# A graph network's count-matrix builder: tiles taken in an order in which heavy and merged ones alternate

## The reference

```
# layer 0: messages weighted by three Gaussians of the edge's attributes, averaged by destination
xj    = x[src] @ g                                   # E x (3*64)
msg   = einsum(xj.reshape(E,3,64), gauss)            # gauss: E x 3
aggr  = segment_sum(msg, dst) / max(count(dst), 1)
x     = layernorm(x + silu(aggr + x @ root_w + bias + x))
# layer 1: two SAGE convolutions over the same edges
h     = relu(x @ W_self1 + (segment_sum(x[src], dst) / deg) @ W_neigh1 + b1)
x     = layernorm(x + h @ W_self2 + (segment_sum(h[src], dst) / deg) @ W_neigh2 + b2)
```

## Time and profile before

| | us |
|---|---|
| median of 3 runs | 7653.07 (7649.23 to 7657.9) |
| the profiled execution | 7651.4 |
| its span, first to last instruction | 7649.6 |
| busy in the span: PE / DVE / POOL / ACT | 5050.4 / 4374.6 / 3367.5 / 2714.0 |
| granted TensorE clock, mean | 0.832 |

### The profile page before, as it was taken

One profiled execution on the slowest core, in us unless ns is written; L12 is line 12 of the kernel. 1 busy time (PEld: TensorE's weight loads), 2 busy tenths in 40 slices (PEclk: granted clock), 3 DMA queues, 4 the chain that ended last, 5 costly groups with the idle time before them and its releaser, 6 DMA issues.

```text
span 7649.6 us, 144672 instructions
## 1 busy us (share of the span) xinstructions
PE 5050.4 (66%) x35195; PEld 4048.2 (53%) x35196; DVE 4374.6 (57%) x15088; ACT 2714.0 (35%) x8317; POOL 3367.5 (44%) x3146
## 2 busy tenths in 40 slices
PE   1565655555566666655555555555545899999999
PEld 1223333333344444444444444444425899999999
DVE  5668888767677777665656656566543322222222
ACT  3113333334444444455555555555532000000000
POOL 5024555555666666666666666666630000000000
PEclk9558888877788888777778888788775899999999
DMA  2001222212222222222222222222230799999998
GB/s 71 28 24 49 68 68 68 67 51 87 78 96 83 87 91 90 90 90 91 90 90 91 91 90 90 73 90 90 91 85 3 298 381 383 381 367 385 385 384 344
DMA packets 258352, 1082.32 MB, mean 141 GB/s; under 512 B 140102, under 2 KB 144230, under 8 KB 194406
## 3 DMA queue, kind: packets, MB, share of 16 engines
q1 hardware_dynamic: 142806, 968.66, 32.8%
q0 software_dynamic: 100352, 102.96, 6.9%
q10 hardware_dynamic: 14902, 8.11, 0.5%
HBM read 751.67 MB, written 327.81 MB: 141 GB/s over the span
## 4 chain that ended last, share of the span: by engine, by line
PE 39%; DVE 20%; issue 14%; DVEq 13%; POOL 5%; DMA 5%; ACT 4%; ACTq 1%; SPq 1%; POOLq 0%
PE pw L970 21%; PE pw L800 9%; DVE rE L1269 5%; POOL rE L512 5%; DVEq L1302 3%; DMA tab<-tab_d 3%; DVEq L1472 3%; PE pw L825 3%; DVE rE L1267 2%; DVE rE L1329 2%; PE pw L772 2%; ACT rE L559 1%; DVE rE L1395 1%; PE pw L937 1%; ACT sca L575 1%
## 5 line engine op out<-in xcount | busy, mean ns | idle before, releaser
L512 POOL DMA_INDIRECT rE<-in_x,idx x3136 | 3365.4, 1073 | 2262.7 <-issue 2092.9
L800 PE MATMUL pw<-rE 128*128 128x193 f32 x7824 | 1775.9, 391 | 921.5 <-DVE rE L1329 885.9
L598 ACT CAST rB<-pw 128x792 bf16<-128x792 f32 x1568 | 1259.6, 814 | 2903.6 <-PE pw L825 1489.4
L800 PEld LDWEIGHTS pw<-rE 128*128 128x128 f32 x7824 | 1623.7, 233 | 1130.5 <-DVE rE L1329 1061.5
L559 ACT ACTIVATE rE<-rE,cols 128x64 f32<-128x64 f32 x4704 | 1254.5, 344 | 8.2 <-DMA tab<-tab_d 8.2
L825 PE MATMUL pw<-rE 128*128 128x396 f16 x3840 | 804.1, 357 | 577.8 <-DVE rE L1269 576.8
L1269 DVE TENSOR_SCALAR rE<-iperm,gr 128x392 f16<-128x392 f16 x3840 | 1052.1, 314 | 0.0
L825 PEld LDWEIGHTS pw<-rE 128*128 128x128 f16 x3840 | 368.8, 103 | 954.4 <-DVE rE L1269 681.1
L970 PE MATMUL pw<-rB,rA 128*128 128x192 bf16 x9604 | 810.8, 246 | 0.1
L970 PE MATMUL pw<-rE,rA 128*128 128x192 bf16 x9604 | 810.4, 246 | 0.1
L970 PEld LDWEIGHTS pw<-rB,rA 128*128 128x128 bf16 x9604 | 790.8, 98 | 1.6
(11 more groups left out here) (256 smaller groups left out, 2626.6 us busy)
## 6 DMA issues: line engine op xcount, KB each, us to landing
rA<-count SPq DMA_DIRECT2D x392, 1568.0 KB, 8.5
count<-rB SPq DMA_DIRECT2D x98, 3136.0 KB
rE<-in_x,idx POOLq DMA_INDIRECT x3136
cols<-cols_d SPq DMA_DIRECT2D x98, 64.0 KB
cols_d<-rA SPq DMA_DIRECT2D x3, 1568.0 KB, 5.2
rA<-in_edge_attr ACTq DMA_DIRECT2D x1, 4608.0 KB
out<-gcol ACTq DMA_DIRECT2D x97, 32.0 KB, 5.8
count<-rB SPq DMA_DIRECT2D x8, 224.0 KB, 2.0
```

The lines of the kernel that those rows point to most:

```text
L512: pool.indirect_dma_start(out=gath[:, s, u * CB + b, :], out_offset=None, in_=x, in_offset=bass.IndirectOffsetOnAxis(ap=idx[:, s, u * CB + ...
L598: act.copy(stage[:, s, :, j * 2 * W:(j + 1) * 2 * W].rearrange("p h (w n) -> p w h n", w=2), pu[j % 3][:, :, 0:CW].rearrange("p w (h n) -> ...
L800: ins = pe.matmul(sums[side][:, 0:AW], onehot[:, side, bb, :], wgath[:, side, bb, :], start=(bb == 0), stop=(bb == CB - 1))
```

## The change

It makes a list `ORDER` of the tiles and lets every engine go through it by place q. In it the 14 heavy tiles alternate with the first 14 merged ones: 0, 1, 2, 48, 3, 49, 4, ... 60, 15, 61, then the single tiles 16 to 47, then the merged tiles 62 to 97. So `q` now sets the slot and the semaphores' values, and `t` the tile. VectorE, TensorE and ScalarE have a loop with a merged and a heavy tile in one turn, 13 times. SyncE's loops are written out, with fixed addresses. Merging needs its own input tile `gm`, since a heavy tile uses `gr` at the same time. `merge_ahead` goes from unit 4 to unit 6 of the tile before, and ScalarE's copies from units 6 to 9 to units 7 to 10. A merged tile behind a heavy one waits at its units 0 to 3 for more of the ring to be free. Two loops of VectorE, that over the single tiles and that over the last merged ones, get `head_slot` 16, which loads the loop's first instruction at slot 16 of a fetch block of 256 instructions; before, 22 and 1 padding instructions stood ahead of them.

```diff
+NI = T4 - DT - 1
+QC = DT + 2 + 2 * NI
+QM = QC + TM - T4
+ORDER = list(range(DT + 1)) + [t for i in range(NI) for t in (TM + i, DT + 1 + i)] + [TM + NI] \
+    + list(range(T4, TM)) + list(range(QM, 98))
...
-            tile_counts(DT, 2, late=False)
-            with dve.Fori(0, T4 - DT - 1, 1) as i:
-                tile_counts(i + (DT + 1), 2)
-
-            dve.wait_ge(a_used, T4 * NU + RU)
-
-            for _ in range(22):
-                dve.sem_inc(s_tick[3], 1)
-            with dve.Fori(0, TM - T4, 1) as i:
-                tile_counts(i + T4, 1)
-            dve.wait_ge(a_pair, TM * NU)
-            merge_ahead(TM)
-            merge(TM)
-            for _ in range(1):
-                dve.sem_inc(s_tick[3], 1)
-            with dve.Fori(0, NT - 1 - TM, 1) as i:
-                merged_counts(i + TM)
-            merged_counts(NT - 1, True)
+            tile_counts(DT, DT, 2, late=False, s=0, following=(TM, 0))
+            with dve.Fori(0, NI, 1) as i:
+                merged_counts(i * 2 + (DT + 1), i + TM, s=1)
+                tile_counts(i * 2 + (DT + 2), i + (DT + 1), 2, s=0, following=(i + (TM + 1), i + 1))
+            merged_counts(QC - 1, TM + NI, s=1)
+            with nc.Fori(0, QM - QC, 1, engines=[dve.engine], head_slot={dve.engine: 16}) as i:
+                tile_counts(i + QC, i + T4, 1)
+            dve.wait_ge(a_pair, QM * NU)
+            merge_ahead(QM, QM, QM - TM, 0)
+            merge(QM - TM)
+            with nc.Fori(0, NT - 1 - QM, 1, engines=[dve.engine], head_slot={dve.engine: 16}) as i:
+                merged_counts(i + QM, i + QM, behind=1, following=(i + (QM + 1), i + (QM + 1 - TM)))
+            merged_counts(NT - 1, NT - 1, s=1, behind=1)
...
-                        dve.wait_ge(a_used, t * NU + (n + 1))
+                        free = n + 1 if behind < 2 else max(n + 1, min(n + 3, 4))
+                        dve.wait_ge(a_used, q * NU + free)
...
+            def merge_between(n, q, following, other):
+                t, m = following
+                if n == 6:
+                    merge_ahead(q + 1, t, m, other)
+                if n == NU - 2:
+                    merge(m)
```

More of the change, by code:

```diff
@@ L384, in _ @@
             sp.sem_inc(a_col, 1)
-            for s in range(2):
-                load_cols(s, s)
+            for q in range(2):
+                load_cols(q)
             for u in range(U):
                 sp.wait_ge(a_g[0][u], 16 * CB)
[L389 to L409, removed]
+            load_idx(2)
             def tile_of(c, t):
@@ L415, in _ @@
                 sp.sem_inc(a_st[s], 1)
[L416 to L420, removed]
-                if end:
-                    after(part, n - 4, 0)
-                    after(part, n - 3, 1, rows=False)
-                    for s in range(2):
-                        after(part, n - 2 + s, s, True, False)
+            for q in range(NT):
+                part = max(k for k, (base, _) in enumerate(PARTS) if ORDER[q] >= base)
+                sp.wait_ge(a_evac, q * NU + (NU + 2))
+                sp.wait_ge(a_bnd, q + 1)
+                sp.dma_start(tile_of(count[part][0], ORDER[q] - PARTS[part][0]), stage[:, q % 2, None, 0:NT, :]).then_inc(a_st[q % 2], 16)
+                if q + 2 < NT:
+                    sp.wait_ge(a_list, q + 1)
+                    load_cols(q + 2)
+                if q + 3 < NT:
+                    for u in range(U):
+                        sp.wait_ge(a_g[1 - q % 2][u], 16 * CB * ((q + 1) // 2 + 1))
+                    load_idx(q + 3)
             sp.wait_ge(e_clr, 1)
@@ L1397, in merged_counts @@
                         if n == 1:
-                            listed(t - 1, slot_of(t + 1) if not isinstance(t, int) else 1 - t % 2)
-                            base_of(t)
+                            listed(q - 1, other)
+                            base_of(q, t)
                         if n % (NU // U) == 1:
-                            prepare(t, s, u)
-                        if n == 4 and not last:
-                            merge_ahead(t + 1)
-                        if n == NU - 2 and not last:
-                            merge(t + 1)
+                            prepare(q, s, u)
+                        if following is not None:
+                            merge_between(n, q, following, other)
                 for k in range(2):
```

157 lines of the change are left out of this document (87 added, 70 removed).

## The result

| | before | after |
|---|---|---|
| median (lowest to highest), us | 7653.09 (7649.23 to 7657.9) | 7420.99 (7416.69 to 7424.71) |
| ratio to before, 95% interval | | 0.9696 [0.9679, 0.9713] |
| the profiled execution, us | 7651.4 | 7416.69 |
| VectorE's `wbase`: heavy and first 14 merged tiles | 871.8 + 671.4 = 1543.2 | 1395.3 |
| first seven single tiles | 426.0 | 402.6 |

The five stretches say where: 148 us in the pairs (forecast: 55 there and 16 further on), 60 in the last merged tiles (forecast: 4), 23 in the first single tiles (forecast: 0), 7.5 in the other single ones.

The account below looks back on a forecast made before the run. VectorE was taken to set the pace in the heavy stretch, GpSimd in the merged one. 7651.4 - 71 (moved merged tiles) - 4 (later `merge_ahead`) = 7576 us, as a median 7578; range 7485 to 7642.

Parts of the forecast that it names:

- VectorE sets the pace in the pairs, GpSimd keeps up: Pairs of heavy and merged tile: 111 us of VectorE against 98.8 us of GpSimd, 12 us to spare.
- A merged tile costs 44 us beside a heavy one: The 14 moved merged tiles: 687 us leave the end, 616 come in beside heavy tiles, 71 us saved.
- once per pair as it was per heavy tile: 0: Loop branch in the pairs: about 2.1 us per turn, paid as often as before, so no change.
- its upper end: Moved merged tile's highest price: 53 us, today's 48.0 plus a 5.2 us wait like the longest at L1394.
- the borders: Rival: turns between heavy and merged tiles cost 8.5 us extra, 110 us against 75 gained: 7688 us; chance 0.07.
- its second rival: Part of the merged tiles' waits closes beside heavy ones: 39 us per tile, 141 us saved, 7512 us; chance 0.16.
- part of the waits closes: Rival: merged tiles at 39 us beside heavy ones, 141 us saved, 7512 us; chance 0.16.
- The last 36 merged tiles: Later `merge_ahead` there: GpSimd sets the pace, so 4 us saved, within bounds of 0 and 45 us.
- Loop heads 0: VectorE's single and last merged loops: new position gains up to 23 us or loses 48; taken as 0.
- The rival of the cached loop: Single loop begun at slot 16 keeps its head cached, branch free: 23 us more saved, 7555 us; chance 0.06.
- Borders cost more than they bring: Rival: branch and TensorE wait add 8.5 us in each of 13 pair turns, 7688 us; chance 0.07.
- the forecast's 71: Saving from moving 14 merged tiles beside heavy ones: 687 us leave the end, 616 come in.

Follow-up runs that it names:

- a_fewg: The changed kernel with only four of a chunk's eight gathers made in the last 36 merged tiles: 7287.06 us, those tiles 44.3 us each.
- b_late3: The kernel before, in its old order, with only `merge_ahead` at unit 6 and ScalarE's copies at units 7 to 10: 7592.96 us, ratio 0.9925.
- a_early2: The changed kernel with `merge_ahead` back at unit 4 and ScalarE's copies at units 6 to 9: 7474.66 us, ratio 0.9766.
- b_heads: The kernel before, in its old order, with `head_slot` 16 on the two loops instead of 22 and 1 padding instructions: 7624.23 us, ratio 0.996.

## Why the prediction was wrong

**VectorE sets the pace in the pairs, GpSimd keeps up: right.** GpSimd's rows show waits for ScalarE and VectorE throughout, and VectorE's busy time did not change.

**A merged tile costs 44 us beside a heavy one ("I take 44: 616 us come in"): this is the step that failed**, and 93 us of the error lie in it: the measured price is (1395.3 - 871.8)/14 = 37.4 us. a_fewg shows that 44 was, within 3 us, the merged tile's price in its old company. By its estimate, 41, those 3 us would be 42 of the 93 and have nothing to do with the heavy neighbour. The other 3.6 us per tile, about 50, come from carrying 44, and the heavy tile's 67.1, to new neighbours unchanged. By line, before to after, in the pairs:

- the tiles' starts, -26 us (69.2 + 52.0 + 0.5 to 5.0 + 64.9 + 26.2; L1384 is the 0.5). That the branch is paid "once per pair as it was per heavy tile: 0" held: 26.1 us at L1384 in the pairs, for the 27 that the prediction read out of the 69.2; and the old merged loop's branch, right ahead of L1384, cost nothing. What was carried over wrongly is the load of the words, 3.2 us of every heavy tile's start. In the pair neither a branch nor a wait for VectorE's own work stands ahead of it, the sequencer does the 1.6 us load while VectorE still has work queued, and the heavy tile starts after 0.15 us. At the merged tile the load stands behind L1384, which waits for the tile before, and is paid in full, and in the pairs always from the slow slot: 4.97 us, where it was 2.03 and 5.15 in turn. Nearly all of L1394's 52.0 us is this load, too (7 x 2.03 + 7 x 5.15 = 50.3): the 5.15 that the profile puts down to TensorE in three of the tiles stand behind a load of 4.7 us as the others do. So the 5.2 us of the earlier trace rows, which the prediction took for a wait for TensorE and used for its upper end and for the borders, were the load, and so were the 15.4 us of its second rival. The merged tiles of before, 3219.4 to 3890.8 us, then one start in order of time, and the load in it (ns):

```profile
L1384 DVE CAST wf<-wi 128x64 f32<-128x64 int32 x14 | 2.8, 197 | 0.5
...
3447.61 0.19 DVE L1384 CAST wf<-wi 128x64 f32<-128x64 int32 x1
3452.96 0.25 DVE L1394 TENSOR_SCALAR rE<-iota_h,wf 128x128 f16<-128x128 f16 x1 [5.15 <-PE pw L819]
...
L1302 DVEq TENSOR_LOAD <-tab x1: 4727/4727/4727, 3448.0 to 3448.0; - x1
```

- L1248, -20 us: 63.6 us for 16 second rounds of a chunk instead of 83.9. TensorE's clock was 0.78 in the old merged stretch and is 0.88 in the pairs, the heavy tiles' level. Busy time per product of the side, (399.5 - 167.4)/1152 = 201 ns instead of 246, if the heavy tiles' share stayed:

```profile
L800 PE MATMUL pw<-rE 128*128 128x193 f32 x1152 | 283.2, 414 | 140.7 <-DVE rE L1329 132.6 <-ACT rE L559 4.8 <-issue 3.2
L800 PE MATMUL pw<-rE 128*128 128x193 f32 x864 | 167.4, 349 | 49.4 <-DVE rE L1329 35.9 <-issue 13.5
```

```profile
L795 PE MATMUL pw<-rE 128*128 128x193 f32 x2016 | 399.5, 355 | 162.6 <-DVE rE L1328 153.6 <-ACT rE L547 8.7
```

(before: merged, heavy; after: pairs). 16 x 45 ns are 0.7 of the 1.3 us that a round became shorter. How much of it is the clock was not isolated: in b_late3 a product of the same 14 tiles took 262.0/1152 = 227 ns, at a mean clock of 0.78 as before.

```profile
L800 PE MATMUL pw<-rE 128*128 128x193 f32 x1152 | 262.0, 391 | 132.4 <-DVE rE L1329 121.9 <-ACT rE L559 7.9 <-issue 2.5
```

- L1459, -24 us: 65.3 became 41.1. The waits for TensorE there went from 30.8 to 10.4; those for ScalarE's copies stayed (34.4 to 30.7).
- L1311 and L1366, -17 us: the waits for ScalarE's sequencer (6.9) and for its copies (8.4) are gone beside a heavy tile.

Together 87 of the 93. The lines are shown; that the neighbour is the cause is shown by the order of instructions for the load, and by a_fewg's estimate for some 50 us of the whole, not for each line. This is near the rival "part of the waits closes", which I gave 0.16 and 39 us per merged tile; measured are 37.4, with the heavy tile's own saving counted in. Of its reasons, the copies not in the way show in the last item; the wait for TensorE at L1394 was a misread load. I weighed the rival against the two 44 us tiles of the earlier trace rows, which were measured among merged neighbours and so could say nothing about it.

**The last 36 merged tiles ("I take 4, since GpSimd hardly waits now"): failed, too,** 50 us by a_early2 and 52 by b_late3. I took GpSimd's 49.1 us per tile for its own. But it is not fixed: with `merge_ahead` at unit 4 a gather took 1052, 1053 and 1056 ns in three kernels, at unit 6 1030 to 1039 in six, and with the idle time ahead of it 1.53 us, (1199.6 + 543.1)/1136, became 1.50, (1174.1 + 526.0)/1130: about 30 us in 35 tiles. The other 22 lie in the last three merged tiles, which took 57.9, 54.4 and 57.5 us before and 49.0, 47.6 and 50.6 after: there VectorE fell behind GpSimd by its waits for the table (11.2 us at the last two) and set the pace itself. The prediction had bounded the term at 45 us, by the pace that moved, and picked the end near nothing. By the rule of the Trainium skill cited there (GPSIMD Engine Reference, Key points) GpSimd and VectorE contend for SBUF interfaces that they share. The 328 and 343 ns of VectorE's instruction in a_fewg and the changed kernel agree with it from VectorE's side. The 20 ns of the gather are no test of it, since VectorE ran the same instructions in both, only at another unit; what causes them was not isolated.

**Loop heads 0: failed by 23 us, and in the direction that had been priced.** The gain that the prediction priced, "23 us" in seven tiles, is what was measured (426.0 to 402.6); it took 0 between this gain and a loss. The rival of the cached loop was true for b_heads. In the new order the head slot is not needed for it.

**Borders cost more than they bring: no.** The wait of the merged tile for the ring (L1395, TensorE) is 0.6 us in 13 turns, as assumed.

**Adding up** the changed stretches against the forecast's terms: 148 - 71 = 77 in the pairs' account (the forecast's 71 includes the 16 us that it expected further on), 56 in the last merged tiles, 23 heads, 7.5 other singles, -5 behind: 158 of the 157 missing.

**The three parts of the change.** On the measured medians: order and the lie of its code about 155 us (7653 to 7474.66 without the later `merge_ahead` is 178, of which 23 are the singles' branch), later `merge_ahead` 50, loop place 23.

## What to carry to other kernels

An instruction group's idle time belongs to its neighbours as much as to itself: when an order is changed, carry over busy time, and price each wait again by who stands beside it, and each load and branch by whether the engine still has work queued when it comes to it. A short wait put down to another engine may be a load of registers: look at the sequencer's own instructions before using it. "The pace of engine X" read from a trace is not X's own until its durations have been seen under another neighbour; here it moved by 2%. And before the order of work is touched, look at the small loads and branches that stand where the pace-setting engine starts a tile: moving the table's second slot by 42 words brought 47 us.

## What the runs showed of the hardware

- A load of 22 words into registers took VectorE's sequencer 1.6 us from a slot at word 0 or 128 of the table's tile and 4.7 us from one at word 86. Why was not isolated.
- The idle time that such a load left on VectorE was 2.03 or 5.15 us behind an instruction that waits, and 0.15 us where the sequencer came to it with work still queued.
- A loop's branch cost VectorE 2.15 us of idle time in the pairs, 2.9 in the single loop of before and none in that loop after it was moved, nor in the merged loop of before (0.03 us).
- A gather of 64 partitions took GpSimd 1035 ns, one of 128 partitions 1039.
- VectorE's `comp` instruction took 343 ns beside 32 gathers per tile and 328 beside 16.
- The same program took 7650 or 8800 to 9030 us, on one and the same chip 7652 and 8797, with single register instructions of ScalarE of up to 1394 ns where they had been at most 160. Why was not found.
